# Splitting projection slots into thirds and weighing half tiles across turns in a channel-attention kernel

## The chip, the cores and the metric

The kernel runs on one core of a Trainium2 chip. The metric is the device time of one execution in microseconds (us), the median of several runs.

## The reference

`x` is 4 x 512 x 48 x 48. It is normalized by groups of 16 channels, and goes through an attention layer of eight heads of 64 channels over the 2304 positions, with a shortcut projection; the result is added to `x`.

```python
x + conv_ref(gn(x), Wq, Wk, Wv, Wsc, gamma)
# conv_ref, n = 2304 positions, 8 heads of 64 channels
q = einsum('bchw,oc->bohw', x, Wq)          # k, v and sc alike
attn = softmax(einsum('bhdn,bhdm->bhnm', q, k), axis=-1)
out = einsum('bhnm,bhdm->bnhd', attn, v)
return gamma * out + sc
```

## The kernel before, in words

**Tiling.** The work is 16 groups (four batches, `b`, times four pairs of heads) of 6 chunks (`c`, 384 queries each): 96 chunks, numbered `n`. A chunk runs over 18 tiles of 128 keys; each is a *turn* `k` of the TensorE loop, and a step `s = 18 n + k`. The two heads of a pair stand on the two halves of the 128 partitions, so nearly every product is a pair of matmuls, one on rows 0 to 63 of the array, one on rows 64 to 127. fp32 accuracy comes from splitting operands into an upper and a lower fp16 or bf16 part.

**A turn of TensorE** (main loop, L550 to L591) issues:

- `score(n, k)` (L447): three pairs of 384 columns into SL. It waits for the exponential of the step before (`s_exp`), since SL holds one step. In turn 0 one more pair adds the shift from CR.
- `top(U)` (L430): one pair of 384 columns into MX, 22 steps ahead, from which VectorE takes the maximum (L795); it waits for the reduction before (`s_mxf`).
- `weigh(s, part)` (L480): the product of the exponentials with V into OB, in two halves (`part` 0 and 1). A half has, for each of three query tiles, a pair with the exponentials' upper part (129 columns, L510) and a pair with their lower part PLO (65 columns, L507). `part` 0 waits for GpSimd's PLO (`s_rest`); between the halves of a step the row groups swap their accumulators, for which `part` 1 waits until the half before it is complete (`s_half`). Part 0 of step 0 of a chunk also waits until OB has been emptied (`s_oe`). Steps are weighed `LAG` = 3 turns late.
- `slot(J, i)` (L384): projections of the next group. A projection unit (`k`, `q`, `v` of 384 positions, or the shortcut `sc`) takes two *blocks* of turns: in block J rows 0 to 63 of the unit begun then, together with rows 64 to 127 of the unit begun in block J - 1. The blocks start at the turns `STARTS` = 0, 4, 8, 13. Each has 12 terms, one slot per term, and `SLOTS` (L60) tells how many slots a turn has. A slot is a pair of 384 columns, or three of 128 for `v` (L379, L381).
- `result(n, rows)` (L407), in turns 11 and 16: six products of 64 columns on one row group, which add the attention's result to the shortcut unit.

**The other engines.** ScalarE takes the exponential into PE32 (L635, five buffers), empties finished units from PJ, empties OB in turn 3 (L642) and divides. VectorE takes maxima, empties units (`leave`), adds the lower part of OB in turn 3 (L807), takes the reciprocal (L814), and in the first group of a batch the statistics of the next batch's x (L941, turns 1, 5, 11, 15). GpSimd makes PLO (L986), lower parts of keys and results (L977, L982), and in pairs 1 and 2 of a batch the lower part of the normalized x (L1063, turns 10, 13, 15, 17, last three chunks of the pair).

**SyncE** issues all DMAs in a loop over chunks (L302 to L323), in order: the x piece for the next batch's statistics or normalization into gx (`load_piece`, L271, one buffer), the x chunk for the sum (`load_x`, L275), the transpose of the maxima (`shift_rows`, L286, which waits for turn 14's `s_cc`), and `store(n - 1)` (L281), which waits until the shortcut unit of chunk n - 1 is finished (`s_pjd`), at the end of chunk n.

Of the kernel before, what the change touches and what calls it, by code (L numbers as in the profile page):

```python
# [12 lines left out]
P = 128  # L13
# [5 lines left out]
CH = 384  # L19
# [40 lines left out]
SLOTS = (3, 3, 3, 3, 3, 3, 3, 3, 3, 2, 3, 2, 2, 3, 2, 3, 2, 2)  # L60
# [3 lines left out]
def block_of(k):  # L64

    b = max(i for i, at in enumerate(STARTS) if at <= k)
    lo = sum(SLOTS[STARTS[b]:k])
    return b, lo, lo + SLOTS[k]

# [49 lines left out]
def build(nc, x, wq, wk, wv, wsc, gamma, out):  # L119
    ctx = ExitStack()  # L120
    with ctx:
# [148 lines left out]
        def _(sp):  # L270
# [14 lines left out]

            def shift_rows(n):  # L286

                sp.wait_ge(s_cc, 2 * n + 2)
                sp.dma_start_transpose(CR[:, :, :], c16[:, :, :].rearrange("p i n -> p (i n)")).then_inc(s_cr, 16)
# [10 lines left out]
            load_x(0)  # L300
            for n in range(CHUNKS):
                g, c = divmod(n, NCH)  # L302
                b, j = divmod(g, PAIRS)
                if j == 0 and b + 1 < BATCH:
                    if c:
                        sp.wait_ge(s_gst, NCH * (b + 1) + c)
                    elif b:
                        sp.wait_ge(s_gno, NCH * b)
                    load_piece(b + 1, c)
# [12 lines left out]
                if n:  # L322
                    store(n - 1)  # L323
# [6 lines left out]
        def _(pe):  # L330
# [38 lines left out]
            def term(u, rows, i, a):  # L369
# [7 lines left out]
                if kind == "v":  # L377
# [3 lines left out]
                return pe.matmul(dst[:, 0:CH], WT[rows, WEIGHT[kind], wp, t, j * P:(j + 1) * P],  # L381
                                 X[rows, b % 2, p, t, c * CH:(c + 1) * CH], **edge)

            def slot(J, i):  # L384

                begun, ended = unit_in(J), unit_in(J - 1)
                if begun and i == 0:
# [3 lines left out]
                if ended and i == 0:  # L391
                    pe.wait_ge(s_low, PLACE[ended] - OPENING + 1)
                low = (QT if begun[0] == "v" else 1) if begun else 0
                high = (QT if ended[0] == "v" else 1) if ended else 0
                for a in range(QT):
                    if a < low:
                        one = term(begun, slice(0, D), i, a)
                        if i == TERMS - 1 and a == low - 1:
                            one.then_inc(s_low, 1)
                    if a < high:  # L400
                        one = term(ended, slice(D, P), i, a)
                        if i == TERMS - 1 and a == high - 1:
                            one.then_inc(s_pj, 1)
# [73 lines left out]
            def weigh(s, part):  # L477
# [17 lines left out]
                for i in range(QT):  # L495
                    for lower in range(2):
# [53 lines left out]
            for n in range(CHUNKS):  # L550
                for k in range(MT):
# [13 lines left out]
                    if lo == 0:  # L565
                        if s >= LAG:
                            weigh(s - LAG, 0)
                        if U < TOPS:
                            top(U)
                        if s >= LAG:  # L570
                            weigh(s - LAG + 1, 0)
                    elif k - 1 in STARTS:
                        if s > LAG:
                            weigh(s - LAG - 1, 1)
                        if U < TOPS:
                            top(U)
                    else:
                        if s >= LAG:
                            weigh(s - LAG, 0)
                        if U < TOPS:  # L580
                            top(U)
                    if n and k in (11, 16):
                        result(n - 1, slice(0, D) if k == 11 else slice(D, P))
                    for i in range(lo, hi):
                        if k == 2 and i == lo + 1 and s >= LAG:
                            weigh(s - LAG, 1)
                        slot(4 * n + b, i)
                    if s > LAG and k != 2 and lo:
                        weigh(s - LAG, 1)
                    if root_unit(n, k):  # L590
                        root(*root_unit(n, k)[1:], U + 1)  # L591
            for s in range(STEPS - LAG, STEPS):
# [158 lines left out]
        def _(dve):  # L751
# [171 lines left out]
            for n in range(CHUNKS):  # L923
                for k in range(MT):
# [166 lines left out]
```

## Time and profile before

| | |
|---|---|
| median of 3 runs | 3061.51 us |
| lowest, highest | 3053.64, 3065.14 us |
| the profiled execution | 3054.18 us, span 3052.5 us |
| TensorE matmuls busy | 2947.1 us (97%), x70175 |
| GpSimd busy | 2746.9 us (90%) |
| VectorE busy | 2010.6 us (66%) |
| ScalarE busy | 1945.1 us (64%) |
| HBM over the span | 25 GB/s |

The profile is of one execution, taken by the hardware profiler; its busy times are shares of the span of 3052.5 us, which is 1.7 us less than that execution's time. Starts in a timeline are microseconds from the span's start. The ends of matmuls are modelled: a row's duration includes the pipeline's depth, so the pace of TensorE is read from the starts of successive rows. Rows of consecutive like instructions are merged, with their count behind the x.

### The profile page before, as it was taken

Reading aid. Unit: us, or ns where it says so; the run is one execution under the profiler, and the core shown is the slowest. Engines: PE = TensorE matmul, PEld = TensorE weight load, DVE = VectorE, ACT = ScalarE, POOL = GpSimd, SP = SyncE. Lnnn points to the kernel's source line nnn. Section 1 sums busy time; section 2 is a strip of 40 time slices with the busy share of each in tenths; the row PEclk is TensorE's granted clock in tenths of the full one; section 3 lists DMA queues with packets and bytes.
Section 4 is the critical chain, followed back from the end, with each engine's and each line's share of the span. In section 5 each row is a group of like instructions: output and inputs, shape, how many; then the busy total and the mean of one; then the engine's idle time right before and its main releaser. Section 6 shows DMA issues by size and latency. Waiting matters only on the chain. (4 is left out here: it accounts for less than half of the span.)

```text
span 3052.5 us, 151591 instructions
## 1 busy us (share of the span) xinstructions
PE 2947.1 (97%) x70175; PEld 2346.8 (77%) x70175; DVE 2010.6 (66%) x2665; ACT 1945.1 (64%) x3156; POOL 2746.9 (90%) x2043
## 2 busy tenths in 40 slices
PE   6999999999999999999999999999999999999999
PEld 4677777878777777887877777787787878878766
DVE  7666666666666666666666666666666666666663
ACT  4566676766565567676666566767666666666555
POOL 2788999999888899999989799999999989999998
PEclk9999999999999999999999999999999999999999
DMA  3110110110111101010001101101000000000000
GB/s 133 32 39 28 31 37 23 38 32 16 33 36 38 31 26 43 16 54 16 23 26 44 46 16 30 39 28 42 20 19 23 16 23 16 23 17 22 17 21 18
DMA packets 93082, 94.15 MB, mean 31 GB/s; under 512 B 44320, under 2 KB 90400, under 8 KB 92448
## 3 DMA queue, kind: packets, MB, share of 16 engines
q1 hardware_dynamic: 92448, 84.44, 9.2%
q8 instruction: 551, 9.03, 1.3%
q14 instruction: 83, 0.68, 0.1%
HBM read 56.10 MB, written 18.87 MB: 25 GB/s over the span
## 5 line engine op out<-in xcount | busy, mean ns | idle before, releaser
L986 POOL TENSOR_TENSOR PLO<-PE 128x768 f16<-128x768 f32 x1727 | 2507.5, 1466 | 244.2 <-ACT PE L635 227.1
L795 DVE TENSOR_REDUCE mx<-MX 128x2 f32<-128x768 f32 x1728 | 1655.6, 958 | 913.0 <-PE MX L445 891.6
L635 ACT ACTIVATE PE<-SL 128x768 f32<-128x768 f32 x1728 | 1400.5, 810 | 986.3 <-PE SL L471 986.3
L510 PE MATMUL OB<-V,PE 64*128 64x129 f16 x20736 | 1450.5, 219 | 11.5 <-POOL PLO L986 10.2
L507 PE MATMUL OB<-V,PLO 64*128 64x65 f16 x20736 | 1356.6, 191 | 0.0
L510 PEld LDWEIGHTS OB<-V,PE 64*128 64x128 bf16 x20736 | 1108.2, 94 | 172.4 <-POOL PLO L986 21.8
L471 PE MATMUL SL<-QK 64*128 64x384 f16 x10368 | 1159.3, 324 | 11.6 <-ACT PE L635 9.4
L507 PEld LDWEIGHTS OB<-V,PLO 64*128 64x128 f16 x20736 | 1013.2, 95 | 139.0 <-issue 1.8
L381 PE MATMUL PJ<-X,WT 64*128 64x384 f16 x6624 | 978.8, 323 | 5.7 <-issue 5.7
L445 PE MATMUL MX<-QK 64*128 64x384 f16 x3456 | 592.6, 325 | 42.1 <-DVE mx L795 40.9
L471 PEld LDWEIGHTS SL<-QK 64*128 64x128 f16 x10368 | 469.2, 94 | 160.1 <-ACT PE L635 19.8
L381 PEld LDWEIGHTS PJ<-X,WT 64*128 64x128 f16 x6624 | 387.2, 94 | 78.6 <-issue 6.7
L379 PE MATMUL PJ<-WT,X 64*128 64x128 f16 x6480 | 429.9, 217 | 0.2 <-issue 0.2
L379 PEld LDWEIGHTS PJ<-WT,X 64*128 64x128 f16 x6480 | 342.7, 94 | 20.4 <-issue 0.4
L445 PEld LDWEIGHTS MX<-QK 64*128 64x128 f16 x3456 | 191.8, 94 | 71.2 <-DVE mx L795 67.5
L651 ACT ACTIVATE attn<-Oe,rc 128x64 f32<-128x64 f32 x570 | 163.9, 337 | 0.0
L977 POOL TENSOR_TENSOR QK<-DF,QK 128x384 f16<-128x384 f32 x96 | 87.7, 913 | 3.8 <-ACT QK L602 3.8
L982 POOL TENSOR_TENSOR half<-attn,half 128x384 f16<-128x384 f32 x95 | 86.8, 913 | 0.0
L618 ACT ACTIVATE QK<-PJ 128x384 f16<-128x384 f32 x93 | 45.6, 490 | 43.9 <-PE PJ L381 38.2
L781 DVE SCALAR_TENSOR_TENSOR xr<-PJ,xr 128x384 f32<-128x384 f32 x96 | 52.5, 547 | 27.1 <-PE PJ L381 27.1
L413 PEld LDWEIGHTS PJ<-identq,half 64*128 64x128 f16 x1140 | 58.0, 95 | 12.9
L941 DVE BATCH_NORM_STATS2 stat<-gx 128x6 f32<-128x384 f32 x72 | 39.8, 553 | 42.7 <-DMA gx<-x 42.7
(109 smaller groups left out, 1013.9 us busy)
## 6 DMA issues: line engine op xcount, KB each, us to landing
gx<-x SPq DMA_DIRECT2D x36, 768.0 KB, 4.9
xr<-x SPq DMA_DIRECT2D x96, 192.0 KB, 2.5
out<-xr SPq DMA_DIRECT2D x96, 192.0 KB, 1.9
X<-x SPq DMA_DIRECT2D x6, 768.0 KB, 8.5
CR<-c SPq DMA_TRANSPOSE x96, 2.4
QK<-wk SPq DMA_DIRECT2D x1, 1024.0 KB, 9.1
QK<-wv SPq DMA_DIRECT2D x1, 1024.0 KB, 11.3
QK<-wq SPq DMA_DIRECT2D x1, 1024.0 KB, 12.0
```

The costliest lines, as they stand in the source:

```text
L379: return pe.matmul(dst[:, a * P:(a + 1) * P], X[rows, b % 2, p, t, m * P:(m + 1) * P], WT[rows, 2, wp, t, j * P:(j + 1) * P], **edge)
L381: return pe.matmul(dst[:, 0:CH], WT[rows, WEIGHT[kind], wp, t, j * P:(j + 1) * P], X[rows, b % 2, p, t, c * CH:(c + 1) * CH], **edge)
L445: last = pe.matmul(MX[:, h, 0:CH], QK[r, g % 2, QH, c * CH + i * P:c * CH + (i + 1) * P], QK[r, g % 2, KH, t * CH:(t + 1) * CH], start=Tru ...
L471: last = pe.matmul(SL[:, h, 0:CH], QK[r, g % 2, a, keys], QK[r, g % 2, b, q], start=False, stop=a == DH and b == QL, skip_group_check=True)
L507: last = pe.matmul(acc[:, 0:AW], PLO[r, s % PB, p0:p0 + P], v[:, 0:AW], start=False, stop=end, skip_group_check=True)
L510: last = pe.matmul(acc, upper, v, start=begin, stop=False, skip_group_check=True)
L635: act.activation(PE32[:, s % PB, :].rearrange("p (h n) -> p h n", h=2), SL[:, :, 0:CH], ACT.Exp, scale=1.0 / SS).then_inc(s_exp, 1)
L651: one = act.activation(attn[:, i * P + h * D:i * P + (h + 1) * D], Oe[:, h, i, 0:D], ACT.Copy, scale=rc[:, h, i, :])
L795: nc.vector.tensor_reduce(mx3[:, n % 2, :, k], MX[:, :, 0:CH], AX.X, ALU.max).then_inc(s_mxf, 1)
L977: nc.gpsimd.tensor_tensor(QK[:, g % 2, DL, c * CH:(c + 1) * CH], DF[:, KCOUNT[u] % 2, :], QK[:, g % 2, DH, c * CH:(c + 1) * CH], ALU.subtr ...
L982: nc.gpsimd.tensor_tensor(half[:, 1, :], attn[:, :], half[:, 0, :], ALU.subtract).then_inc(s_al, 1)
L986: nc.gpsimd.tensor_tensor(PLO[:, s % PB, :], PE32[:, s % PB, :], PE32[:, s % PB, :].bitcast(BF16)[:, 1:4 * CH:2], ALU.subtract).then_inc(s ...
```

## The change

- **Projection in thirds.** `THIRDS` replaces `SLOTS`: the share of a turn is counted in thirds of a term (128 of its 384 columns), and `thirds(J, lo, hi)` replaces `slot(J, i)`. A term that is cut is issued as a pair of 256 and a pair of 128 columns, each with its own weight load. Blocks have 9, 9, 5, 13 / 9, 9, 9, 9 / 8, 8, 8, 5, 7 / 8, 8, 8, 5, 7 thirds.
- **Half tiles across turns.** The first half of step s - 3 is weighed at the end of turn s, behind the projection (in turns 4, 8, 13 and 0 before it), and the second half in the next turn behind the scores. In turn 2 both halves of the last step of the chunk before are weighed; turn 3 has one half alone.
- **Order in a half.** The three pairs with the upper part come first, then the three with the lower part.
- **First keys of a batch.** The wait for all six normalized x pieces becomes, for each key unit, a wait for its own piece.
- **SyncE.** The statistics load of chunk n + 1 is issued in chunk n, behind the transpose and ahead of the store.
- **VectorE.** In turn 3 the reciprocal comes behind the emptying of a unit.

```diff
-SLOTS = (3, 3, 3, 3, 3, 3, 3, 3, 3, 2, 3, 2, 2, 3, 2, 3, 2, 2)
+THIRDS = (9, 9, 5, 13, 9, 9, 9, 9, 8, 8, 8, 5, 7, 8, 8, 8, 5, 7)
...
+            def stats_piece(n):
+                g, c = divmod(n, NCH)
+                b, j = divmod(g, PAIRS)
+                if j == 0 and b + 1 < BATCH:
+                    if c:
+                        sp.wait_ge(s_gst, NCH * (b + 1) + c)
+                    elif b:
+                        sp.wait_ge(s_gno, NCH * b)
+                    load_piece(b + 1, c)
...
                 if n + 1 < CHUNKS:
                     shift_rows(n + 1)
+                stats_piece(n + 1)
                 if n:
                     store(n - 1)
...
-                        pe.wait_ge(s_gno, NCH * (begun[1] // PAIRS))
+                        pe.wait_ge(s_gno, NCH * (begun[1] // PAIRS - 1) + begun[2] + 1)
...
+                for i in range(lo // 3, (hi + 2) // 3):
+                    first, end = max(lo - 3 * i, 0), min(hi - 3 * i, 3)
+                    for a in range(first, end):
+                        last = i == TERMS - 1 and end == 3
+                        if begun and (a == first or begun[0] == "v"):
+                            one = term(begun, slice(0, D), i, a, end)
...
-                for i in range(QT):
-                    for lower in range(2):
+                for lower in range(2):
+                    for i in range(QT):
...
                     if k == LAG:
+                        thirds(4 * n + b, lo, lo + 7)
                         if U < TOPS:
                             top(U)
-                        slot(4 * n + b, lo)
-                        slot(4 * n + b, lo + 1)
+                        thirds(4 * n + b, lo + 7, hi)
                         weigh(s - LAG, 0)
-                        slot(4 * n + b, lo + 2)
-                        weigh(s - LAG, 1)
                         continue
...
+                    if s > LAG:
+                        weigh(s - LAG - 1, 1)
+                    if k == LAG - 1 and n:
+                        weigh(s - LAG, 0)
+                    if U < TOPS:
+                        top(U)
+                    if lo == 0 and s > LAG:
+                        weigh(s - LAG, 0)
...
+                    if k == LAG - 1:
+                        thirds(4 * n + b, lo, lo + 3)
+                        if n:
+                            weigh(s - LAG, 1)
+                        thirds(4 * n + b, lo + 3, hi)
+                        continue
+                    thirds(4 * n + b, lo, hi)
+                    if lo and s > LAG:
+                        weigh(s - LAG, 0)
...
-                    if k == LAG and n:
-                        invert(n - 1)
                     if k == 4 and n and root_unit(n - 1, MT - 1) and root_unit(n - 1, MT - 1)[2] == 1:
                         root_invert(root_unit(n - 1, MT - 1)[1])
                     if done_at(s):
                         leave(done_at(s))
+                    if k == LAG and n:
+                        invert(n - 1)
```

TensorE, turn 3 of chunk 6, before (SL scores, MX maximum, PJ projection, OB weighing):

```order
L471 MATMUL SL<-QK 128x384 x6
L445 MATMUL MX<-QK 128x384 x2
L381 MATMUL PJ<-X,WT 128x384 x4
L510 MATMUL OB<-V,PE 128x129 x2
L507 MATMUL OB<-V,PLO 128x65 x2
...
L381 MATMUL PJ<-X,WT 128x384 x2
L510 MATMUL OB<-V,PE 128x129 x2
L507 MATMUL OB<-V,PLO 128x65 x2
```

and the same turn in the changed kernel, with the first rows of turn 4:

```order
L477 MATMUL SL<-QK 128x384 x6
L386 MATMUL PJ<-X,WT 128x128 x2
L386 MATMUL PJ<-X,WT 128x384 x4
L451 MATMUL MX<-QK 128x384 x2
L386 MATMUL PJ<-X,WT 128x384 x4
L516 MATMUL OB<-V,PE 128x129 x6
L513 MATMUL OB<-V,PLO 128x65 x6
L477 MATMUL SL<-QK 128x384 x6
L516 MATMUL OB<-V,PE 128x129 x6
L513 MATMUL OB<-V,PLO 128x65 x6
```

The turn had two halves, each alternating upper and lower pairs; now it has 13 thirds and one half at its end, uppers first, and the second half stands behind the next scores.

SyncE, chunks 1 and 2, before (gx statistics load, xr load, CR transpose, out store):

```order
L284 DMA out<-xr 128x384 [waits s_pjd]
L273 DMA gx<-x 128x4x384 [waits s_gst]
L279 DMA xr<-x 128x384 [waits s_st0]
L289 DMA_TRANSPOSE CR<-c 128x3x128 [waits s_cc]
L284 DMA out<-xr 128x384 [waits s_pjd]
```

and in the changed kernel:

```order
L273 DMA gx<-x 128x4x384 [waits s_gst]
L284 DMA out<-xr 128x384 [waits s_pjd]
L279 DMA xr<-x 128x384 [waits s_st0]
L299 DMA_TRANSPOSE CR<-c 128x3x128 [waits s_cc]
L273 DMA gx<-x 128x4x384 [waits s_gst]
```

The statistics load has moved from behind the store to ahead of it, right behind the transpose.

## Rows read from the trace of the kernel before

**Rows 1.** Timeline of SP: start us, us, engine, line, operation. The transposes at ten chunks.

```profile
143.12 1.19 SPq L289 DMA_TRANSPOSE CR<-c  x1
...
271.11 1.19 SPq L289 DMA_TRANSPOSE CR<-c  x1
...
366.40 1.19 SPq L289 DMA_TRANSPOSE CR<-c  x1
...
518.29 1.19 SPq L289 DMA_TRANSPOSE CR<-c  x1
...
639.58 1.19 SPq L289 DMA_TRANSPOSE CR<-c  x1
...
672.21 1.18 SPq L289 DMA_TRANSPOSE CR<-c  x1
...
822.08 1.19 SPq L289 DMA_TRANSPOSE CR<-c  x1
...
1022.31 1.19 SPq L289 DMA_TRANSPOSE CR<-c  x1
...
1574.42 1.92 SPq L289 DMA_TRANSPOSE CR<-c  x1
...
1773.39 1.19 SPq L289 DMA_TRANSPOSE CR<-c  x1
```

**Rows 2.** Timeline of turn 9 of chunk 80: TensorE, then ScalarE's exponential.

```profile
2584.82 0.66 PE L471 MATMUL SL<-QK 64*128 64x384 f16 x6
2585.31 0.23 PE L510 MATMUL OB<-V,PE 64*128 64x129 f16 x2
...
2585.57 0.33 PE L445 MATMUL MX<-QK 64*128 64x384 f16 x2
...
2586.38 0.66 PE L471 MATMUL SL<-QK 64*128 64x384 f16 x6
...
2585.51 0.81 ACT L635 ACTIVATE PE<-SL 128x768 f32<-128x768 f32 x1 [0.44 <-PE SL L471]
```

**Rows 3.** Timeline of turn 3 of chunk 80: TensorE, then VectorE's part of the evacuation.

```profile
2574.67 0.69 PE L471 MATMUL SL<-QK 64*128 64x384 f16 x6
...
2575.72 0.23 PE L510 MATMUL OB<-V,PE 64*128 64x129 f16 x2
...
2576.22 0.23 PE L510 MATMUL OB<-V,PE 64*128 64x129 f16 x2
...
2576.50 0.33 PE L471 MATMUL SL<-QK 64*128 64x384 f16 x2
...
2575.10 0.56 DVE L807 TENSOR_TENSOR Oe<-OB,Oe 128x384 f32<-128x384 f32 x1
```

**Rows 4.** Statistics loads: the wait in the list of waits, then timelines (SP, VectorE, TensorE).

```profile
DVE stat L941 <- DMA gx<-x: 42.7, 16, 3.7
...
115.56 0.58 SPq L273 DMA_DIRECT2D gx<-x  x1
...
180.64 0.72 SPq L273 DMA_DIRECT2D gx<-x  x1
...
185.46 0.56 DVE L941 BATCH_NORM_STATS2 stat<-gx 128x6 f32<-128x384 f32 x1 [2.29 <-DMA gx<-x]
...
186.93 0.34 PE L445 MATMUL MX<-QK 64*128 64x384 f16 x2 [1.83 <-DVE mx L795]
```

**Rows 5.** Timelines of GpSimd in chunk 8, TensorE there, and GpSimd in chunk 18.

```profile
361.70 5.75 POOL L986 TENSOR_TENSOR PLO<-PE 128x768 f16<-128x768 f32 x4
...
363.22 0.23 PE L510 MATMUL OB<-V,PE 64*128 64x129 f16 x2 [1.27 <-POOL PLO L986]
...
646.60 0.91 POOL L1063 TENSOR_TENSOR X<-gx,X 128x384 f16<-128x384 f32 x1
```

**Rows 6.** Timeline of TensorE at the result products in turn 11: weight loads, products.

```profile
1015.74 0.34 PEld L413 LDWEIGHTS PJ<-identq,half 64*128 64x128 f16 x5
1015.89 0.28 PE L413 MATMUL PJ<-identq,half 64*128 64x64 f16 x4
```

More of the change, by code:

```diff
@@ L66, in block_of @@
     b = max(i for i, at in enumerate(STARTS) if at <= k)
-    lo = sum(SLOTS[STARTS[b]:k])
-    return b, lo, lo + SLOTS[k]
+    lo = sum(THIRDS[STARTS[b]:k])
+    return b, lo, lo + THIRDS[k]
 def unit_in(J):
@@ L300, in _ @@
             load_x(0)
+            stats_piece(0)
             for n in range(CHUNKS):
[L302 to L309, printed above, removed]
+                b = n // NCH // PAIRS
                 if norm_piece(n) is not None:
@@ L367, in project, with term @@
                     last.then_inc(s_pj, 1)
-            def term(u, rows, i, a):
+            def term(u, rows, i, a, end):
                 kind, dst = u[0], bank(u)
@@ L380, in term @@
                                      WT[rows, 2, wp, t, j * P:(j + 1) * P], **edge)
-                return pe.matmul(dst[:, 0:CH], WT[rows, WEIGHT[kind], wp, t, j * P:(j + 1) * P],
-                                 X[rows, b % 2, p, t, c * CH:(c + 1) * CH], **edge)
-            def slot(J, i):
+                return pe.matmul(dst[:, a * P:end * P], WT[rows, WEIGHT[kind], wp, t, j * P:(j + 1) * P],
+                                 X[rows, b % 2, p, t, c * CH + a * P:c * CH + end * P], **edge)
@@ L386, in slot, with thirds @@
+            def thirds(J, lo, hi):
                 begun, ended = unit_in(J), unit_in(J - 1)
-                if begun and i == 0:
+                if begun and lo == 0:
                     left(same_bank_before(begun))
                     if begun[0] == "k" and begun[1] % PAIRS == 0:
-                        pe.wait_ge(s_gno, NCH * (begun[1] // PAIRS))
-                if ended and i == 0:
+                        pe.wait_ge(s_gno, NCH * (begun[1] // PAIRS - 1) + begun[2] + 1)
+                if ended and lo == 0:
@@ L392, in slot @@
                     pe.wait_ge(s_low, PLACE[ended] - OPENING + 1)
[L393 to L403, printed above, removed]
+                for i in range(lo // 3, (hi + 2) // 3):
[4 more added lines that the diff above has]
+                            one = term(begun, slice(0, D), i, a, end)
+                            if last and (begun[0] != "v" or a == 2):
+                                one.then_inc(s_low, 1)
+                        if ended and (a == first or ended[0] == "v"):
+                            one = term(ended, slice(D, P), i, a, end)
+                            if last and (ended[0] != "v" or a == 2):
+                                one.then_inc(s_pj, 1)
@@ L556, in _ @@
                     if k == LAG:
+                        thirds(4 * n + b, lo, lo + 7)
                         if U < TOPS:
                             top(U)
-                        slot(4 * n + b, lo)
-                        slot(4 * n + b, lo + 1)
+                        thirds(4 * n + b, lo + 7, hi)
                         weigh(s - LAG, 0)
-                        slot(4 * n + b, lo + 2)
-                        weigh(s - LAG, 1)
                         continue
[L565 to L581, printed above, removed]
+                    if s > LAG:
+                        weigh(s - LAG - 1, 1)
@@ L582, in _ @@
+                    if k == LAG - 1 and n:
[4 more added lines that the diff above has]
+                        weigh(s - LAG, 0)
                     if n and k in (11, 16):
                         result(n - 1, slice(0, D) if k == 11 else slice(D, P))
-                    for i in range(lo, hi):
-                        if k == 2 and i == lo + 1 and s >= LAG:
+                    if k == LAG - 1:
+                        thirds(4 * n + b, lo, lo + 3)
+                        if n:
@@ L586, in _ @@
                             weigh(s - LAG, 1)
-                        slot(4 * n + b, i)
-                    if s > LAG and k != 2 and lo:
-                        weigh(s - LAG, 1)
+                        thirds(4 * n + b, lo + 3, hi)
[3 more added lines that the diff above has]
+                        weigh(s - LAG, 0)
                     if root_unit(n, k):
                         root(*root_unit(n, k)[1:], U + 1)
+            weigh(STEPS - LAG - 1, 1)
```

## The prediction

> **What bounds the kernel now.** I read the chunk clock first, then one turn, then the stalls. The chunk clock is the transpose that SyncE issues once per chunk, late in the chunk before. The five chunks from 672.21 to 822.08 take 149.87 us, so a plain chunk of 18 turns takes 30.0 us [rows 1]. Over 96 chunks that is 2880 us of the 3052.5 us span; the rest is the opening, the tail, and stalls that I price below.
>
> Inside a plain turn TensorE has no rest. In turn 9 [rows 2] the scores begin at 2584.82, the first half weighing at 2585.31 (scores 0.49), the products for the maximum at 2585.57 (a half 0.26), and the next scores at 2586.38. One pair of 384-column products is a third of the scores, 0.163, and so are a projection slot and the maximum's pair. Turn 9 has two slots: 0.49 + 2 x 0.26 + 0.163 + 0.325 = 1.50 us of work, but it lasts 1.56. The difference is a second loop: the exponential starts 0.69 after the scores (2585.51), lasts 0.81, and the next scores start 0.06 after its end, 1.56 in all [rows 2]. So TensorE sets a turn of three slots (1.66), and the loop through ScalarE sets a turn of two.
>
> **1. Thirds.** Before, the last two blocks have turns of 3, 2, 3, 2, 2 slots; now 8, 8, 8, 5, 7 thirds. Four turns of a chunk (9, 12, 14, 17) have two slots and no other cover; each loses 0.06 to the loop: 0.24 us. Now 8 thirds give 1.175 + 8 x 0.054 = 1.61, above the floor, and 7 thirds give 1.56, at it. Turns 11 and 16 carry the six result products (0.03 each, 0.17 in all) beside 5 thirds: 1.62. The same work is spread so that no turn waits: 0.24 saved. Seven cuts fall inside a term, and each adds one pair with its weight load. A pair's fixed part is at most what a 64-column product takes beyond nothing, 0.03 [rows 6], and at least zero; I take 0.003 (0.163 for three thirds against 0.057 for one of 129 columns, worked out under 4), 0.02 per chunk.
>
> **2. Turn 3.** Here the accumulator OB of the chunk before is emptied. The turn runs from 2574.67 to 2576.50, 1.83 us, with work of 0.49 + 0.163 + 3 x 0.163 + 0.52 = 1.66 [rows 3]. It loses 0.10 at the first half, which starts at 2575.72, 0.06 after VectorE finished Oe (2575.10 + 0.56), and 0.07 at the second, which starts 0.50 after the first with only 0.26 + 0.163 of work between: it waits for the first half to be complete, because the row groups swap accumulators. Now the first half comes after 13 thirds and the maximum, 0.49 + 0.71 + 0.163 = 1.36 into the turn, and the second half in the next turn behind 0.49 of scores. In turn 2 the last half is issued later (1.34 into the turn, before 1.08, since two halves come ahead of the maximum) and the turn grows to 1.71. Oe is then ready 1.28 into turn 3, against the 1.36 at which it is wanted: a margin of 0.08, the thinnest of the change. Turn 3 becomes 1.62, turn 2 grows by 0.04: 0.165 saved, if the margin holds. VectorE's own load is unchanged; the reduction of turn 3 starts about 1.26 into it, so the projection's result leaves PJ about 1.06 into turn 4, where 1.175 is wanted. Moving the reciprocal (L814) behind that departure keeps this second margin; I cost it at nothing.
>
> Parts 1 and 2 give 0.24 + 0.165 - 0.04 (turn 2) - 0.02 = 0.345 per chunk; as two margins are thin I take 0.31, times 96: **30 us**, with 0.15 and 0.38 as ends (14 to 36).
>
> **3. Waits of the weighing for GpSimd.** Before, at the starts of blocks the half of step s-2 is weighed 0.92 into the turn; now no step is weighed before turn s+3, late. The slack after GpSimd's natural end grows from about 1.2 us to 2.6 or more (GpSimd takes 1.42 per step back to back: four in 5.75 with the last at 1.47 [rows 5]). The 1.27 us wait at 363.22 [rows 5] is of this kind, once in each of three chunks (8, 32, 56): 4 us. The chunks in which GpSimd also writes X pieces show it too: the five from 366.40 to 518.29 take 1.9 us more than 150, the three from 548.3 (518.29 plus one plain chunk) to 639.58 1.3 more [rows 1]: 3.2, three times, 9.5 us. GpSimd needs 18 x 1.42 + 5 x 0.88 = 30.0 us in such a chunk against TensorE's 29.7, so a backlog of 0.3 per chunk grows for three chunks, under the slack; I leave 1 us. **12.5 us**, between 6 (GpSimd stays the bound there) and 13.5. Delaying the second half delays the release of a PE32 buffer, but it is still issued a turn before the exponential that needs it.
>
> **4. Order in a half.** The same six pairs. The results' stream shows 64-column products on one row group 0.03 apart, each with its own weight load ((0.28 - 0.19) / 3 [rows 6]); the upper product is then (0.26 - 3 x 0.03) / 3 = 0.057. A lower product's weights load today behind an upper one (0.057) and an upper's behind a lower (0.03); so 0.03 is already enough for a pair of loads, for both row groups at once. **0 us**; ends: 0.005 gained per half (17 us over 3456 halves), and the rival below. The Trainium skill (TensorE: Matmul & The Clock Gate, Back-to-back issue gap) says that in a real stream of weight loads and products the spacing at 128 columns is about 81 ns. By that a half of six pairs would be 0.49 us as an estimate, before and after; the trace has 0.26, so the rule does not hold for these row-tiled pairs.
>
> **5. Statistics loads.** In chunk 3 the load is issued at 180.64, behind the store, which waits for the shortcut unit at the end of the chunk; VectorE stands 2.29 us, from 183.17 to 185.46, before the statistics; the maximum's products then start 1.83 late [rows 4]. The one load not behind a store, at 115.56, precedes its chunk, and nobody waited for it: 16 waits, 42.7 us in all, are the other 16 loads of this kind in pair 0 (2 of 18 do not wait). The load now stands behind the transpose and the wait for the previous statistics (turn 15), and ahead of the store. That puts it about 3.7 us earlier (chunk 3: at about 176.9), landing at about 181.7, 1.4 us ahead of need. The store only comes behind a wait that ends in turn 15, and it waits for turn 17 anyway: no cost. In chunk time the 16 cases cost 127.99 - 120 = 8.0 (143.12 to 271.11), 200.23 - 180 = 20.2 (822.08 to 1022.31) and 198.97 - 180 = 19.0 (1574.42 to 1773.39) [rows 1]: **47 us**, ends 40 (some loads land late) and 47.
>
> **6. X piece by piece.** The first key unit of a new batch waits for all six pieces; the last is written by GpSimd at 646.60 to 647.5 [rows 5], and that chunk takes 32.63 us (639.58 to 672.21 [rows 1]), 2.6 over plain, three times. Now it waits for piece 0, written two pairs earlier: **7.5 us**, ends 6 and 8.
>
> **The sum.** 30 + 12.5 + 0 + 47 + 7.5 = 97 us. The profiled execution took 3054.2 (span 3052.5), so it becomes 2957; it lies 7 us below the median of the runs, 3061.5, and at the lower edge of their 11 us of spread. I forecast 2961, between 2957 and 3061.5 - 97 = 2964.5. What stays: the three sets of root products and table loads in chunks 6 to 8, the opening and the tail.
>
> **Rivals.** *The turns give nothing back:* the late half in turns 2 and 3, or VectorE's reductions, become the new wait. For it: the margins of 0.08 and about 0.1. Against: each is one wait in 18 turns, and the loop's 0.06 in four turns goes regardless. Only parts 3, 5 and 6 then count: 67 us, 2990.
> *The loads still land late,* because the transpose and the load now share the DMA engines, or the load goes no earlier than the store did. For it: the wait on turn 15's statistics. Against: the load at 115.56, issued in just this order. 2961 + 47 = 3008.
> *Slower: weight loads come out from behind three short products.* If a lower product hides the next load only when it is an upper one's length, as each lower one's load has today, the second and third cost 0.057 instead of 0.029: 0.056 x 3456 = 193 us, and 2961 + 193 = 3154. The recorded load of 0.10 bounds it above: 0.07 twice per half, 480 us. It decides from 0.028 per half, where the 97 us are gone. Against: the results' stream at 0.03 with a load each [rows 6], and both row groups' loads behind one lower product today.
> The Trainium skill (the same page, Part 3: Packing small matmuls) says that a weight load overlaps products in flight only when the row group differs. Strictly taken, that is this rival; the results' stream, all on one row group, speaks against it.
>
> **Chances.** The forecast 0.82 (2943 to 2978), no gain from the turns 0.09, late loads 0.03, weight loads 0.04, something that leaves the time as it was 0.02. A measurement of this kernel can tell about 0.5% from no change. Faster by over 0.5% in the first three: 0.94; same 0.02; slower 0.04. The range takes the forecast's own ends (17 us for a gain in part 4, the low ends of 1, 3 and 5) and the first rival: 2942 to 2992.
>
> **What would show it.** Right: plain chunks 29.7 apart on the transposes; turns 9 and 14 at 1.61 and turn 3 at 1.62; VectorE's wait for gx gone and the load issued ahead of the store; the chunk at a batch's first key unit like its neighbours; six products of 65 columns 0.03 apart. Wrong: halves over 0.27 (weight loads), a wait of TensorE for Oe or PJ in turns 3 and 4, or of VectorE for gx in turn 1.

## The result, and the profile after

| | before | after |
|---|---|---|
| median of 4 runs | 3059.49 us | 2946.45 us |
| lowest, highest | 3053.64, 3065.14 us | 2945.93, 2948.15 us |
| the profiled execution's span | 3052.5 us | 2945.1 us |
| TensorE matmuls busy | 2947.1 us (97%) | 2891.6 us (98%) |
| GpSimd busy | 2746.9 us (90%) | 2741.3 us (93%) |

The ratio of the times is 0.9632, with a 95% interval of 0.9612 to 0.9651: the changed kernel is faster by 113 us. The forecast was 2961 us, in a range of 2942 to 2992. The sum of the terms was 97 us, and the two profiled spans differ by 107.4. So the direction and most of the size were right, and about 10 us came from somewhere that the sum had too small.

The chunk clock first. The timeline of SyncE in the changed kernel, the transposes at the same chunks as in [rows 1], as far as they carry the comparison:

```profile
143.12 1.19 SPq L299 DMA_TRANSPOSE CR<-c  x1
...
261.58 1.19 SPq L299 DMA_TRANSPOSE CR<-c  x1
...
354.26 1.19 SPq L299 DMA_TRANSPOSE CR<-c  x1
...
620.72 1.19 SPq L299 DMA_TRANSPOSE CR<-c  x1
...
650.52 1.19 SPq L299 DMA_TRANSPOSE CR<-c  x1
...
798.37 1.19 SPq L299 DMA_TRANSPOSE CR<-c  x1
...
975.77 1.19 SPq L299 DMA_TRANSPOSE CR<-c  x1
```

Each pair of rows is one term of the sum:

| stretch | chunks | before [rows 1] | after | saved |
|---|---|---|---|---|
| plain | 5 (672.21 / 650.52 on) | 149.87 | 147.85 | 2.02, 0.40 each |
| first statistics loads | 4 (143.12 on) | 127.99 | 118.46 | 9.53 |
| second set of them | 6 (822.08 / 798.37 on) | 200.23 | 177.40 | 22.83 |
| X pieces written by GpSimd | 9 (366.40 / 354.26 on) | 273.18 | 266.46 | 6.72 |
| third set of them, rows not shown | 6 (1574.42 / 1512.82 on) | 198.97 | 177.38 | 21.59 |
| first key unit of a batch | 1 (639.58 / 620.72 on) | 32.63 | 29.80 | 2.83 |
| the wait of 1.27 of [rows 5], rows not shown | 1 (332.23 / 321.91 on) | 34.17 | 32.35 | 1.82 |

The stretches with X pieces, with a first key unit and with the 1.27 wait come once in each of three batches. A plain chunk takes 29.57 instead of 29.97 us, and a chunk with a statistics load is now no longer than a plain one: 118.46 / 4 = 29.6, 177.40 / 6 = 29.6.

One turn next. Timeline of TensorE and of ScalarE's exponential in turn 9 of chunk 80, to set beside [rows 2]:

```profile
2482.82 0.70 PE L477 MATMUL SL<-QK 64*128 64x384 f16 x6
2483.31 0.38 PE L516 MATMUL OB<-V,PE 64*128 64x129 f16 x6
2483.48 0.27 PE L513 MATMUL OB<-V,PLO 64*128 64x65 f16 x5
2483.57 0.32 PE L451 MATMUL MX<-QK 64*128 64x384 f16 x1
...
2483.74 0.64 PE L386 MATMUL PJ<-X,WT 64*128 64x128 f16 x8
2484.17 0.38 PE L516 MATMUL OB<-V,PE 64*128 64x129 f16 x6
...
2484.44 0.32 PE L477 MATMUL SL<-QK 64*128 64x384 f16 x1
...
2483.55 0.81 ACT L634 ACTIVATE PE<-SL 128x768 f32<-128x768 f32 x1 [0.38 <-PE SL L477]
```

The turn runs from 2482.82 to 2484.44, 1.62 us, and 1.61 was forecast. The eight thirds are four pairs (of 128, 384, 384 and 128 columns) that take 0.43, from 2483.74 to 2484.17. A half still takes 0.26 (2483.31 to 2483.57). The six upper products (three pairs) stand together in 0.17, and the six lower ones in 0.09, thus 0.03 per pair. The exponential ends at 2484.36, 0.08 before the next scores: TensorE now sets this turn.

Turn 3 of the same chunk, TensorE and VectorE, to set beside [rows 3]:

```profile
2472.93 0.68 PE L477 MATMUL SL<-QK 64*128 64x384 f16 x6
...
2474.29 0.39 PE L516 MATMUL OB<-V,PE 64*128 64x129 f16 x6
...
2474.55 0.32 PE L477 MATMUL SL<-QK 64*128 64x384 f16 x1
...
2473.58 0.56 DVE L806 TENSOR_TENSOR Oe<-OB,Oe 128x384 f32<-128x384 f32 x1
```

The turn lasts 1.62 instead of 1.83. The half starts 1.36 into it, as worked out, and Oe was ready at 2473.58 + 0.56 = 2474.14, so the margin is 0.15, where 0.08 was forecast.

The statistics load of chunk 3, in SyncE's timeline, to set beside [rows 4]:

```profile
172.64 1.19 SPq L299 DMA_TRANSPOSE CR<-c  x1
174.40 0.38 SPq L273 DMA_DIRECT2D gx<-x  x1
177.63 0.34 SPq L284 DMA_DIRECT2D out<-xr  x1
```

The load goes out 3.23 ahead of the store. The list of waits of the changed kernel shows what is left for TensorE inside the chunks (us in total, times, longest us):

```profile
PEld SL L477 <- ACT PE L634: 17.9, 39, 1.8
PEld MX L451 <- DVE mx L794: 12.6, 22, 1.5
PE SL L477 <- ACT PE L634: 11.8, 33, 1.7
...
PE MX L451 <- DVE mx L794: 6.1, 9, 1.1
...
PEld OB L516 <- POOL PLO L985: 1.2, 5, 0.2
```

VectorE's wait for gx is no longer in it, TensorE's weight loads wait for the maximum 12.6 us in 22 places, before 67.5 in 112. Of TensorE's waits for GpSimd's PLO, 21.8 us (weight loads) and 10.2 us (products) before, 1.2 us of the weight loads' is left.

### The profile page after: what moved, and what is told of

Its sections match the earlier page's. It is cut to its first block and busy times, and to the rows that moved or that the text cites. A ratio compares the mean times of both kernels' runs of the same rounds, so it can differ in the third digit from the quotient of the medians.

```text
span 2945.1 us, 153693 instructions
## 1 busy us (share of the span) xinstructions
PE 2891.6 (98%) x71226; PEld 2434.3 (83%) x71226; DVE 2015.9 (68%) x2665; ACT 1949.7 (66%) x3156; POOL 2741.3 (93%) x2043
## 5 line engine op out<-in xcount | busy, mean ns | idle before, releaser
L516 PE MATMUL OB<-V,PE 64*128 64x129 f16 x20736 | 1256.3, 218 | 0.8
L516 PEld LDWEIGHTS OB<-V,PE 64*128 64x128 bf16 x20736 | 1004.5, 94 | 220.5 <-DVE Oe L806 3.0
L513 PE MATMUL OB<-V,PLO 64*128 64x65 f16 x20736 | 983.8, 191 | 0.0
L386 PE MATMUL PJ<-X,WT 64*128 64x384 f16 (+2 forms) x7675 | 983.1, 301 | 0.0
L513 PEld LDWEIGHTS OB<-V,PLO 64*128 64x128 f16 x20736 | 740.3, 95 | 0.0
L477 PEld LDWEIGHTS SL<-QK 64*128 64x128 f16 x10368 | 483.2, 94 | 126.4 <-ACT PE L634 17.9
L386 PEld LDWEIGHTS PJ<-X,WT 64*128 64x128 f16 x7675 | 453.4, 94 | 73.3 <-issue 0.3
L451 PEld LDWEIGHTS MX<-QK 64*128 64x128 f16 x3456 | 207.7, 93 | 18.2 <-DVE mx L794 12.6
L641 ACT ACTIVATE Oe<-OB 128x390 f32<-128x390 f32 x96 | 47.7, 497 | 31.8 <-PE OB L513 31.8
L1062 POOL TENSOR_TENSOR X<-gx,X 128x384 f16<-128x384 f32 x72 | 66.3, 921 | 0.0
```

Source lines behind the costliest of these rows:

```text
L386: return pe.matmul(dst[:, a * P:end * P], WT[rows, WEIGHT[kind], wp, t, j * P:(j + 1) * P], X[rows, b % 2, p, t, c * CH + a * P:c * CH + e ...
L451: last = pe.matmul(MX[:, h, 0:CH], QK[r, g % 2, QH, c * CH + i * P:c * CH + (i + 1) * P], QK[r, g % 2, KH, t * CH:(t + 1) * CH], start=Tru ...
L477: last = pe.matmul(SL[:, h, 0:CH], QK[r, g % 2, a, keys], QK[r, g % 2, b, q], start=False, stop=a == DH and b == QL, skip_group_check=True)
L513: last = pe.matmul(acc[:, 0:AW], PLO[r, s % PB, p0:p0 + P], v[:, 0:AW], start=False, stop=end, skip_group_check=True)
L516: last = pe.matmul(acc, upper, v, start=begin, stop=False, skip_group_check=True)
```

## The experiments

The kernel before had medians of 3055.7 to 3057.9 us beside these runs, with a spread of about 11 us; the kernels built on the changed one spread by 1 to 6 us, so they are compared with the changed kernel directly: 2946.45, and 2946.09 when it ran again beside runs 7, 9 and the second of 10. Runs 1, 2, 4 and 5 were on another chip than the rest; the kernel before differs by at most 2.2 us between the two.

**1. The order in a half.** The changed kernel with upper and lower products in alternation again:

```diff
-                for lower in range(2):
-                    for i in range(QT):
+                for i in range(QT):
+                    for lower in range(2):
```

> The changed kernel, with upper and lower products alternating within a half again. Theory (the order is worth nothing): 2946 us, within 3, since a half lasts 0.26 either way. Rival (the order is part of the 10 us by which the change beat the sum): about 5 ns per half come back, 2946 + 3456 x 0.005 = 2963.

Measured: 2947.82 us (2946.47 to 2948.62). The order is worth nothing that these runs can tell (1.4 us with overlapping ranges), which is part 4's 0 us. The rival in which weight loads come out from behind the short products wanted 193 us; it falls.

**2. The statistics load back behind the store.**

```diff
-            stats_piece(0)
             for n in range(CHUNKS):
                 b = n // NCH // PAIRS
+                stats_piece(n)
...
-                stats_piece(n + 1)
```

> The changed kernel, with the statistics load at its old place behind the store. Theory: 16 stalls of VectorE for gx return, 42 to 47 us, 2989 to 2993. Rival (faster turns and the larger slack hide a part of the late loads): under 35 us, below 2981.

Measured: 2982.64 us (2979.33 to 2984.86), 36 us more. That lies between the two expectations. VectorE's wait is back at full size, and TensorE pays less of it than before. From the list of waits and the timelines of this run (chunk 3):

```profile
DVE stat L939 <- DMA gx<-x: 40.8, 16, 3.5
...
181.45 0.35 SPq L284 DMA_DIRECT2D out<-xr  x1
181.84 0.43 SPq L273 DMA_DIRECT2D gx<-x  x1
...
186.52 0.56 DVE L939 BATCH_NORM_STATS2 stat<-gx 128x6 f32<-128x384 f32 x1 [2.15 <-DMA gx<-x]
...
188.00 0.34 PE L450 MATMUL MX<-QK 64*128 64x384 f16 x2 [1.27 <-DVE mx L793]
```

VectorE stands 2.15 (before 2.29 [rows 4]), but the maximum's products are only 1.27 late, before 1.83: they come behind seven thirds in the new turn 3, so a part of the stall is covered by work. The other part is the clock. In the kernel before, six of these stalls were followed by a stretch in which the granted clock was 0.50; here three were. In chunk time over a plain chunk, the ten others cost 2.1 each before (31.7 to 32.7 us) and the thirteen others here 1.7; the chunks with the halved clock cost 4.5 each before (33.7 to 35.2) and 4.2 here. Of the difference (48 us in chunk time before, 34 here) about half is the covered work and half the three halved clocks fewer. So the price of a late load depends on the kernel around it, and taking the part out of the new kernel is not the mirror of putting it into the old one. That called for the next run.

**3. The early load alone, in the kernel before.**

```diff
                 if n + 1 < CHUNKS:
                     shift_rows(n + 1)
+                stats_piece(n + 1)
                 if n:
                     store(n - 1)
```

> The kernel before with one part of the change alone: the statistics' load issued behind the transposes and ahead of the store. Theory: the 16 late loads cost 47 us (8.0 + 20.2 + 19.0 in chunk time), all of it goes, so about 3059 - 47 = 3012, VectorE has no wait for gx left and chunks of pair 0 come 30.0 apart. Rival, from the run in which the changed kernel lost only 36 us with the old load: here too only some 36 go, 3023, because part of the 47 is something else that stays.

Measured: 3011.39 us (3008.28 to 3014.08) against 3055.74, a ratio of 0.9852 (0.9836 to 0.9869): 44 us, 40 to 50 by the interval. The theory's 3012 holds, the rival's 3023 does not. In chunk time the three sets take 119.93, 180.31 and 179.96 us, where [rows 1] have 127.99, 200.23 and 198.97: 47.0 us, the term of the sum. The interval of the 44 holds it.

The trace of this run also shows the clock by itself. The wait for all X pieces is still in it, and TensorE stands 1.90 us at each of the three; two of the three rows, and the windows of 2 us behind them (columns: busy of TensorE's products, of its loads, of VectorE, ScalarE, GpSimd, then the granted clock, DMA share and GB/s):

```profile
639.64 0.66 PE L386 MATMUL PJ<-X,WT 64*128 64x384 f16 x6 [1.90 <-issue]
...
2102.72 0.66 PE L386 MATMUL PJ<-X,WT 64*128 64x384 f16 x6 [1.90 <-issue]
...
640.00:642.00 2.00, 2.00 (x46) 1.53 (x44) 0.74 (x1) 0.81 (x1) 1.25 (x2) 1.00 0.32 94
...
2103.00:2105.00 2.00, 2.00 (x28) 1.41 (x24) 0.00 (x0) 0.68 (x1) 1.05 (x1) 0.58 0.23 80
```

The chunks take 32.64, 32.63 and 34.28 us. The standstill is the same in all three; behind the third the granted clock is low, and the chunk is 1.6 longer.

**4. Whole terms in the last two blocks.**

```diff
-THIRDS = (9, 9, 5, 13, 9, 9, 9, 9, 8, 8, 8, 5, 7, 8, 8, 8, 5, 7)
+THIRDS = (9, 9, 5, 13, 9, 9, 9, 9, 9, 6, 9, 6, 6, 9, 6, 9, 6, 6)
```

> The changed kernel with whole terms in the last two blocks (9, 6, 9, 6, 6 thirds twice). Theory: four turns of a chunk fall to the loop of 1.56 us again, 0.22 per chunk: 2946 + 21 = 2967. Rival (the thirds are worth nothing, the gain of the turns is all in where the halves are weighed): 2946.

Measured: 2968.94 us (2966.95 to 2970.04), 22.5 more, 0.23 per chunk. Part 1 had 0.24 - 0.02.

**5. The wait for all six X pieces.**

```diff
-                        pe.wait_ge(s_gno, NCH * (begun[1] // PAIRS - 1) + begun[2] + 1)
+                        pe.wait_ge(s_gno, NCH * (begun[1] // PAIRS))
```

> The changed kernel with the wait for all six x pieces before a batch's first key unit. Theory: GpSimd now writes the last piece later against TensorE than before, about 5 us into the chunk where it is wanted at 1.3, so three waits of some 3.7 us: 2957. Rival: the waits of before, 2.5 each: 2954.

Measured: 2961.61 us (2960.52 to 2964.12), 15 us more, 5.1 to 5.2 in each of three chunks (the one at 620 takes 34.87 instead of 29.80). The part was priced at 7.5, and as a gain over the kernel before that is right (2.83 less the 0.40 of every chunk, three times: 7.3). Undone in the faster kernel it costs double. The timeline of TensorE there, and the windows of 2 us around it (columns as above):

```profile
629.27 1.14 PE L386 MATMUL PJ<-X,WT 64*128 64x384 f16 x6 [3.70 <-issue]
...
628.00:630.00 2.00, 0.73 (x6) 0.47 (x8) 0.00 (x0) 0.00 (x0) 2.00 (x3) 0.73 0.28 91
630.00:632.00 2.00, 2.00 (x26) 1.27 (x24) 0.00 (x0) 0.59 (x1) 0.59 (x1) 0.50 0.00 0
632.00:634.00 2.00, 2.00 (x52) 1.59 (x50) 0.96 (x1) 0.62 (x2) 1.47 (x1) 0.92 0.04 8
```

TensorE stands 3.70 us, since it reaches the wait earlier in relation to GpSimd's last piece. Then its granted clock is 0.50 of full speed from 630 to 632: 26 products lie in these two microseconds, and 52 in the next two. Of the 5.07, 3.70 is the standstill; the 1.37 that is left goes with the halved clock.

**6. Half tiles weighed where they were before.** Thirds in the last two blocks stay.

```diff
-THIRDS = (9, 9, 5, 13, 9, 9, 9, 9, 8, 8, 8, 5, 7, 8, 8, 8, 5, 7)
+THIRDS = (9, 9, 9, 9, 9, 9, 9, 9, 8, 8, 8, 5, 7, 8, 8, 8, 5, 7)
...
                     if k == LAG:
-                        thirds(4 * n + b, lo, lo + 7)
                         if U < TOPS:
                             top(U)
-                        thirds(4 * n + b, lo + 7, hi)
+                        thirds(4 * n + b, lo, lo + 6)
                         weigh(s - LAG, 0)
+                        thirds(4 * n + b, lo + 6, hi)
+                        weigh(s - LAG, 1)
                         continue
...
+                    if lo == 0:
+                        if s >= LAG:
+                            weigh(s - LAG, 0)
+                        if U < TOPS:
+                            top(U)
+                        if s >= LAG:
+                            weigh(s - LAG + 1, 0)
...
```

> The changed kernel with the halves weighed where they were before (both of a block's last and first step inside the turn, 9, 9, 9, 9 thirds in the first block, both halves inside turn 3); thirds in the last two blocks, loads, X pieces, the order in a half and the reciprocal as changed. Theory: turn 3 is back at 1.82 and turn 2 at 1.67, 0.16 x 96 = 15 us, and the waits for GpSimd come back, 12.5 us: 2946 + 28 = 2974. Rival: the later halves also cured the waits at turn 13 in every chunk with a key unit (0.08 to 0.1 each), then up to 6 us more, 2980; or GpSimd's waits are covered by the new room elsewhere, 2961.

Measured: 2987.41 us (2986.43 to 2989.76), 41 us more, past both expectations. TensorE waits for GpSimd more than it did in the kernel before. From the list of waits of this run, and from TensorE's timeline in turn 0 of chunk 11:

```profile
PEld OB L516 <- POOL PLO L994: 34.3, 80, 1.6
...
PE OB L516 <- POOL PLO L994: 12.6, 20, 1.4
...
424.42 0.35 PE L516 MATMUL OB<-V,PE 64*128 64x129 f16 x6 [0.51 <-POOL PLO L994]
```

Before, the same two waits had 21.8 us in 61 places and 10.2 in 20. Faster turns brought TensorE sooner to the half that is weighed early at a block's start, and GpSimd did not get there sooner. By the starts of the scores, summed over all chunks, the changed kernel is 19.4 us shorter than this one in turn 3 and 4.5 longer in turn 2, as the theory had it (15 in both); in turns 0 and 13, the starts of two blocks, it is 11.7 and 16.8 shorter, 28 us where 12.5 was expected.

**7. Neither: early halves and whole terms.** The kernel of run 6 with the table (9, 9, 9, 9, 9, 9, 9, 9, 9, 6, 9, 6, 6, 9, 6, 9, 6, 6).

> The kernel with halves where they were before, now also with whole terms (3 or 2 slots in a turn): only the loads, the X pieces, the order in a half and the reciprocal remain of the change. Thirds were worth 22.5 us with the later halves in place. If thirds and later halves are independent, they are worth as much here: 2987 + 22.5 = 3010. If faster turns only bring GpSimd's waits out while the halves are early (turn 13 and the chunks at 30.55 stay as long as they were), thirds give little here, 5 to 15 us: 2992 to 3002.

Measured: 3000.66 us (2999.38 to 3001.97). With runs 4 and 6 and the changed kernel this makes a square:

| | whole terms | thirds | thirds give |
|---|---|---|---|
| halves early | 3000.66 | 2987.41 | 13.3 |
| halves late | 2968.94 | 2946.09 | 22.9 |
| late halves give | 31.7 | 41.3 | |

Together 54.6 us, of which 9.6 belong to neither alone. They go to the start of a block. TensorE in turn 13 of chunk 80, in the kernel before:

```profile
2591.29 0.66 PE L471 MATMUL SL<-QK 64*128 64x384 f16 x6
...
2592.05 0.33 PE L445 MATMUL MX<-QK 64*128 64x384 f16 x2
...
2592.27 0.10 PEld L510 LDWEIGHTS OB<-V,PE 64*128 64x128 bf16 x2 [0.15 <-POOL PLO L986]
...
2593.04 0.33 PE L471 MATMUL SL<-QK 64*128 64x384 f16 x2
```

The half that is weighed early, behind the maximum's products, waits for GpSimd's PLO, and the turn takes 1.75. Averaged over the 18 chunks from 72 on, by the starts of the scores, turn 13 takes

| turn 13, us | whole terms (three) | eight thirds |
|---|---|---|
| halves early | 1.716 | 1.719 |
| halves late | 1.673 | 1.616 |

With early halves the third of a term that leaves turn 13 (0.05) makes it no shorter. In the first three chunks of each six, GpSimd writes the lower part of a key unit in turn 12 (0.92 from 2589.88 here), PLO comes later by it, and turn 13 even grows, from 1.76 to 1.82; in the other three chunks it falls from 1.67 to 1.62. Over all chunks the thirds give 5.0 us in turn 13 beside late halves and take 2.4 beside early ones, 7.4 of the 8.5 that the starts of the scores have between the two.

The chunks in which GpSimd also writes X pieces show the same, in SyncE's timeline of three of them. The kernel with early halves and thirds:

```profile
388.03 1.19 SPq L299 DMA_TRANSPOSE CR<-c  x1
...
479.79 2.14 SPq L299 DMA_TRANSPOSE CR<-c  x1
```

The kernel with early halves and whole terms:

```profile
388.51 1.19 SPq L299 DMA_TRANSPOSE CR<-c  x1
...
480.27 2.09 SPq L299 DMA_TRANSPOSE CR<-c  x1
```

The kernel with late halves and whole terms (run 4):

```profile
387.26 1.72 SPq L299 DMA_TRANSPOSE CR<-c  x1
...
476.65 1.18 SPq L299 DMA_TRANSPOSE CR<-c  x1
```

The changed kernel:

```profile
383.89 1.19 SPq L299 DMA_TRANSPOSE CR<-c  x1
...
472.87 1.90 SPq L299 DMA_TRANSPOSE CR<-c  x1
```

These are 91.76, 91.76, 89.39 and 88.98 us. With early halves the thirds give nothing at all in these chunks: what TensorE gains in its turns it stands in front of GpSimd. With late halves they give 0.41 in the three.

**8. Short lower products.** The changed kernel with narrower lower products.

```diff
-                                last = pe.matmul(acc[:, 0:AW], PLO[r, s % PB, p0:p0 + P], v[:, 0:AW], start=False,
+                                last = pe.matmul(acc[:, 0:33], PLO[r, s % PB, p0:p0 + P], v[:, 0:33], start=False,
```

> The changed kernel in which each lower product covers 33 of the 65 columns of values: the rest of the lower product, and its part of the column of sums, is left out. It asks what sets the 0.029 between lower products. If their 65 columns do (65 / 2.4 = 27 ns), the pitch falls towards 14 to 16 ns and a half loses up to 0.04: turns of three slots lose 0.08, but turns at the exponential's floor of 1.56 lose nothing beyond it, so some 50 to 100 us less, 2850 to 2900. If loading the weights does, the pitch stays at 0.029 and so does the time: 2946.

Measured: 2909.82 us (2909.11 to 2910.67), 37 less, between the two. Nearly half of the columns went, and a lower pair fell from 0.029 to about 0.025 only: a plain chunk takes 29.10 instead of 29.58 (four chunks from the transposes), 0.48 over 36 halves is 0.0133 each, 0.0044 per lower pair. The columns alone would have taken half of 0.029. In turns 5 to 7, which TensorE sets in both kernels, a turn falls by 0.032 (1.669 to 1.637), thus 0.005 per lower pair. So at 33 columns something other than the columns sets the pace, at 0.024 to 0.025 per pair. It may be the loading of weights, since every product here has its own load, or a fixed part of a product; the run does not separate them. The pairs with 65 columns take 0.004 to 0.005 more than that.

The 37 us are less than 0.48 x 96 = 46, because TensorE waits for GpSimd again in the chunks around the X pieces: 15.1 us in 53 places for its weight loads (1.2 us in the changed kernel), and the chunk from 438.50 to 468.53 takes 30.0 instead of 29.8.

**9. The reciprocal ahead of the departure.** The changed kernel with VectorE's order in turn 3 as before.

```diff
+                    if k == LAG and n:
+                        invert(n - 1)
                     if k == 4 and n and root_unit(n - 1, MT - 1) and root_unit(n - 1, MT - 1)[2] == 1:
                         root_invert(root_unit(n - 1, MT - 1)[1])
                     if done_at(s):
                         leave(done_at(s))
-                    if k == LAG and n:
-                        invert(n - 1)
```

> The changed kernel with the reciprocal of the row sums ahead of the projection's departure from PJ again, as before the change. It tests the second thin margin (1.06 against 1.175 into turn 4). Theory: the reciprocal pushes the departure back by its own length, TensorE waits for PJ in turn 4 of each chunk for what the margin does not hold, 0.05 to 0.1: 5 to 10 us, 2951 to 2956. Rival: the departure is early enough in any case and the moved reciprocal does nothing: 2946.

Measured: 2947.06 us (2946.64 to 2948.06), 1 us more. By the starts of the scores, turn 4 of plain chunks grows by 0.03 (1.67 to 1.70), and about as much comes back in turns 8 to 12 and 17 behind it (0.01 in turns 9 and 11). The rival is right on the time: this part of the change is worth nothing that can be told.

**10. The root's products behind the next scores.** Where a unit of the root ends a chunk, its products are issued behind the first scores of the next chunk.

```diff
                     score(n, k)
+                    if k == 0 and n and root_unit(n - 1, MT - 1):
+                        root(*root_unit(n - 1, MT - 1)[1:], U)
...
-                    if root_unit(n, k):
-                        root(*root_unit(n, k)[1:], U + 1)
```

> The changed kernel with the root's products of a chunk's last turn issued behind the next chunk's first scores instead of ahead of them. Theory: chunks 6 and 7 (and their two later copies) are 0.95 over a plain chunk because the scores stand behind the root's products and the exponential behind the scores; behind the scores only the products' own length remains, 0.3: 6 x 0.6 = 3.6 us less, 2943. Rival: the 0.95 comes from ScalarE's or VectorE's root work, then nothing changes.

> The root's products behind the next chunk's scores once more, now beside the changed kernel on one chip. The first run had 2942.0 with the changed kernel's 2946.45 of another call. Theory: 3.6 to 4.5 us below the changed kernel. Rival: they differ by the chip alone, 0 to 1 us.

> The changed kernel itself, on the chip of the three that follow, so that they are compared with it and not only with the kernel before. Expected: 2946, as before.

Measured: 2942.00 us (2941.75 to 2942.51), and a second time 2942.46 (2942.06 to 2942.70) beside the changed kernel's 2946.09 (2945.39 to 2948.61) on the same chip. The ranges do not touch: 3.6 us. SyncE's timeline of the second of these runs over the three chunks that the changed one takes 92.68 us for (261.58 to 354.26):

```profile
261.11 1.19 SPq L299 DMA_TRANSPOSE CR<-c  x1
...
352.45 1.19 SPq L299 DMA_TRANSPOSE CR<-c  x1
```

91.34, so 1.34 less, three times 4.0. This version is faster than both kernels of the study; against the kernel before it has a ratio of 0.9622 (0.9606 to 0.9638).

## Why the prediction was right, and where its sum was short

The time lies inside the range, but not by the terms that were right. The profiled executions differ by 107.4 us, and the upper ends of the terms that brought a gain (36, 13.5, 47 and 8) add up to 104.5. The range reached down to 2942 because of 17 us that part 4 might gain; it gained nothing, and waits that the sum did not have took their place. That the measured time was inside is in this respect luck; the mechanisms were right, one of them too small.

**What bounds the kernel** held for most turns: TensorE sets turns of more than two slots, and the loop through ScalarE turns 9 and 14 (1.56 before, 1.62 after, 1.61 forecast). Turns 12 and 17, the two behind the result products, did not fit: by the starts of the scores, with turn 0 counted from its shift products, they took 1.63 and 1.66 before, not 1.56, and 1.61 and 1.63 after, not 1.56. No run tells what holds them.

**Part 1, thirds: right.** 0.24 less 0.02 per chunk was the term, and run 4 has 0.23. That is beside late halves; beside early ones run 7 against run 6 has 0.14.

**Part 2, turn 3: right, and subtracted once too often.** Turn 3 went from 1.83 to 1.62 and turn 2 grew by 0.045. The text worked out "0.165 saved" with turn 2's growth in it, and then took the 0.04 off again in the line that adds parts 1 and 2. Rightly added it is 0.385, not 0.345. The step down to 0.31 for thin margins had no row behind it: the margin at Oe is 0.15, and run 9 shows that a reciprocal set into the one at PJ costs 0.03 in turn 4 and nothing in the whole.

**Part 3, waits for GpSimd: the mechanism right, its extent too small.** What was priced came: the X chunks give 6.72 less 9 x 0.40, thus 3.1, where 3.2 less 0.3 was expected, and the chunk with the wait of 1.27 gives 1.82 less 0.40, three times 4.3, priced at 4. But the wait was counted only where whole chunks stood out of the row. It was also inside plain ones, at turn 13, where the early half of a block's start stood: 0.04 us when the turns have whole terms (1.716 against 1.673, the table of run 7), 0.10 when they have thirds (1.719 against 1.616), averaged over chunks with and without a key unit. The prediction took 30.0 as the measure of a plain chunk, so what the plain chunks lost alike could not be seen in it. This is the step that was short.

**Parts 1 to 3 together** were 42.5 us in the sum; run 7 against the changed kernel has 54.6. By the starts of the scores, summed over all chunks (55.6 in all), from run 7 to run 4 to the changed kernel:

| | in the sum | measured |
|---|---|---|
| thirds | 0.22 per chunk, 21 | 22.6 |
| turns 2 and 3 | 0.125 per chunk, 12 | 19.2 - 4.9 = 14.3 |
| waits for GpSimd | 12.5 | 9.4 in turn 0, 9.3 in turn 13 |
| discount for margins | -3 | |

Of the 9.3 in turn 13, 4.4 are the three long waits that were priced, and 5 are the short ones that were not. So the missing 12 are the 0.04 subtracted twice (4 us), the discount (3 us) and the short waits at turn 13 (5 us). That the parts need each other was not seen either: thirds are worth 13.3 us with early halves, 22.9 with late ones. The parts were priced as if independent; the price of the thirds came out right because the late halves were made with them, and this too is luck.

**Part 4, order: right.** A half takes 0.26 in either order. The rule of the Trainium skill (TensorE: Matmul & The Clock Gate, Part 3: Packing small matmuls) that a weight load overlaps products in flight only when the row group differs does not price this kernel: run 1 and the grouped order agree within 1.4 us. Run 8 bounds how near the rival was: if loads set the pace at 33 columns, it was 0.004 to 0.005 per lower pair away.

**Part 5, loads: right.** 47.0 in chunk time alone in the kernel before, 44 (40 to 50) in the runs. The load was to go out about 3.7 earlier; it goes 3.23 ahead of its store and nobody waits. What the text did not say is what the 47 consist of: standing, and a halved clock behind six of the 16 stalls. Around one of them in the kernel before, the maximum's products wait 2.48 us, until 898.68, and from 900 to 902 the granted clock is 0.50. In the changed kernel the granted clock is 1.00 from 94 to 2940 us.

**Part 6, X pieces: right** (7.3 for 7.5); taken out of the changed kernel the part costs 15 us (run 5).

**What the sum left out with the other sign:** the opening and the tail lost a little. From the start to the third transpose both kernels take 143.12 us, though two chunks in it are 0.4 shorter each; from the last transpose to the end it is 42.5 us instead of 41.9.

**Of the rivals**, that the turns give nothing back falls to the table of run 7, late loads to the list of waits and to run 3, and exposed weight loads to run 1.

## What to carry to other kernels

A stall that most periods have alike is invisible in a comparison of periods: look inside the standard period at each turn against its own work, above all at the turns that begin a block. Before adding up parts that lie on the same two engines, ask of each what it is worth without the other; a faster turn in front of an engine that is as late as before gives its gain to the wait. And price a stall of TensorE of two or three microseconds with the clock that may fall behind it: 1.6 us beside a standstill of 1.90 in run 3, in one case of three.

## What was not expected of the hardware

- **The clock behind a stall.** A standstill of 3.70 us cost 5.07 (run 5): the granted clock was 0.50, the lower of its two levels (1.2 against 2.4 GHz), from 630 to 632, when TensorE was already busy again. Not every stall was followed by it: six of 16 in the kernel before, three of 16 in run 2, and one of three in run 3, where all three lasted 1.90 us. The six followed stalls of 2.0 to 3.3 us, the ten others were of 1.6 to 2.6, so the length alone does not tell.
- **Row groups run out of step.** In turn 9 above, the first product of the maximum starts at 2483.57, before the last lower product of the half:

```profile
2483.59 0.19 PE L513 MATMUL OB<-V,PLO 64*128 64x65 f16 x1
2483.62 0.32 PE L451 MATMUL MX<-QK 64*128 64x384 f16 x1
```

By the kernel's order of issue it comes behind it; it is on rows 0 to 63, the lower product on rows 64 to 127. The changed kernel's trace has this order of starts in 583 places. So TensorE's starts need not be in the order of issue across the two row groups.
- **Half of the columns, nearly the same time.** A pair of products with 128 columns of weights takes 0.029 with 65 columns of values and 0.024 to 0.025 with 33 (run 8).
